# Which 128 rows of the input one load brings in: 16 images by 8 rows each, or 128 neighbouring rows of one stride

## The chip, the core and the metric

The kernel runs on one core of a Trainium2 chip. The metric is the device time of one execution, in microseconds (us); lower is better. The core has a matrix engine (PE), a vector engine (DVE), a scalar engine (ACT), GpSimd (POOL) and a queue engine (SP), which issues most of the transfers. Sixteen DMA engines move the data.

## The reference

The input is x, 128 images of 12 channels of 224 x 224 float32. What is computed, cut to what matters here:

```
pooled = x.reshape(B, 12, 14, 16, 14, 16).sum(axis=(3, 5))      # 16 x 16 patches
h = einsum('bcij,ce->bije', pooled, channel_weights)            # 196 tokens of 192 per image
h = h + attention(layernorm(h))       # 64 query tokens on the other 132
h = h + mixture_of_experts(layernorm(h))   # 8 experts, top 2, and a shared one
```

All of x (308 MB) is read once, and only its patch sums are used after that. The output is 128 x 196 x 192 float32.

## The kernel before, in words

**Groups and tiles.** The images go in 8 groups of 16 (`GB`). One group has 16 x 12 x 14 strips, a strip being 16 image rows of one channel, 3584 floats or 14,336 bytes that lie together in memory. A *unit* is (image, channel, half), where the half `s` says whether a strip is among the upper 7 or the lower 7 of its channel. Two neighbouring units, in the order (image, channel, half), lie 25,088 floats apart, over the border between channels and between images too. A *tile* is 128 units at one strip number `i` of 0 to 6: 128 partitions of 14,336 bytes, 1792 KB. A group has `TILES` = 21 tiles, numbered `t = 7k + i` with `k` of 0 to 2 (`CG`), 168 in all. Two buffers hold them (`xt`, `SLOTS` = 2).

**A tile's way.** `load` on SP issues tile t + 2 once DVE, ACT and POOL have all read tile t, which lies in the same buffer. Each of the three sums some of the tile's 14 patches: DVE in one reduction (`dve_tile`, L766), ACT patch by patch (`act_tile`, L626), POOL by a tree of additions (`pool_tile`, L556, L551, L562) that DVE finishes (`finish_rows`, L773). The sums go to `pooled[:, k, :]`.

**From sums to tokens.** Once all 21 tiles of a group are summed, PE transposes the three slices of `pooled` (item `tok`) and DVE copies them from PSUM to `Ptok`, laid out as unit (half, image) by channel. Item `V` multiplies the same slices by `blockG`, a block-diagonal matrix, built once before the groups from `bmask` (1 where a partition belongs to a unit column) and `repG` (`rep` says which channel a partition is). `rep` and `bmask` are made by POOL with memsets and affine selects. After this nothing depends on how a tile's rows were chosen.

**The order of the work.** First comes preparation of the weights (`PREP`), between which the tiles of group 0 are summed (`tiles_after`), one tile for each one or two steps. Then comes a pass for group 0's attention and gates, whose steps also take 19 tiles of group 1; `PLAN` lists the items of a step and `LATE0` its tile. Then each group's experts run in 63 steps on PE, DVE and ACT (`ffn_pe`, `ffn_dve`, `ffn_act`). In their gaps, by `PLAN`, stand the items of the next group, and by `EARLY` and `LATE` the tiles of that group and the one after. Each engine works its list strictly in order, so an engine that waits for a tile holds up the expert step behind it. SP's order is also fixed: it holds the loads, the stores of the output and, near the start, 8 + 9 small copies that spread the channel weights (`CWr_src`, `CWx`).

Of the kernel before, what the change touches and what calls it, by code (L numbers as in the profile page):

```python
# [31 lines left out]
NB, CH, IMG, PATCH = 128, 12, 224, 16  # L32
# [6 lines left out]
GB = 16  # L39
NG = NB // GB  # L40
CG = 3
HALF = NP // 2
HT = HALF * NP
UNITS = 2 * GB
# [179 lines left out]
def build(nc, x, cw, proj_w, proj_b, gate_w, gate_b, w1, w2, w3, sw1, sw2, sw3, out):  # L224
    ctx = ExitStack()
    with ctx:
# [28 lines left out]
        xt = sb("xt", [128, SLOTS, ROW])  # L255
# [16 lines left out]
        Ptok = sb("Ptok", [HT, UNITS, CH])  # L272
        V = sb("V", [HT, UNITS, CH + 1])
        val = sb("val", [HT, UNITS, CH + 1])
# [4 lines left out]
        PHT = sb("PHT", [128, 2, 4, HT])  # L279
# [11 lines left out]
        h = [ffn[:, i, :] for i in range(HR)]  # L291
# [21 lines left out]
        cres = h2q[0:UC, 4, :]  # L313
        CWcT = [rq[:, 0:3, :].rearrange("p a b -> p (a b)")[:, 0:CH], gs[:, 3, 0:CH]]
        G13 = sums[0:CH, :, :].rearrange("p a b -> p (a b)")[:, 0:CH + 1]
        rep = val[0:CH, :, :].rearrange("p a b -> p (a b)")[:, 0:CG * 128].rearrange("p (k n) -> p k n", k=CG)
        repG = gs[:, :, :].rearrange("p a b -> p (a b)")[:, 0:CG * (CH + 1)].rearrange("p (k c) -> p k c", k=CG)
        bmask = PHT[:, 0, 0, 0:UNITS]
        rmask = gt[0:8 * CH, 0, 0:8]
        wres = attw[0:CH, 2 * EX * INTER:2 * EX * INTER + 1024]  # L320

# [30 lines left out]
        pool_link = sem("pool_link")  # L352
        pe_passed, dve_passed = sem("pe_passed"), sem("dve_passed")

        xv = x.rearrange("(g b) (k c) (s i h) w -> g k i b (c s) (h w)", b=GB, k=CG, s=2, h=PATCH)


        PREP = [("CWcT", 0), ("CWcT", 1), ("G", 0), ("gate", 0), ("repG", 0), ("gate", 1)]
# [52 lines left out]
        @block.sync  # L411
        def _(sp):

            sp.dma_start(CWn, cw).then_inc(cw_in, 16)
            sp.wait_ge(const_done, 1)
            sp.dma_start(CW14[CH + 1:UC, :], proj_b.rearrange("(a d) -> a d", a=1)).then_inc(pb_in, 16)
            for k, (w, shared) in enumerate(((w1, sw1), (w3, sw3))):
                sp.dma_start(w13_nat[:, k * EX:k * EX + NE, :], w.rearrange("e i d -> i e d")).then_inc(w_in, 16)
                sp.dma_start(w13_nat[:, k * EX + NE, :], shared).then_inc(w_in, 16)
            for nat, a, b in ((w2_natA, 0, 128), (w2_natB, 128, D)):  # L420
                sp.dma_start(nat[:, 0:NE, :], w2[:, a:b, :].rearrange("e d i -> d e i")).then_inc(w_in, 16)
                sp.dma_start(nat[:, NE, :], sw2[a:b, :]).then_inc(w_in, 16)
            sp.dma_start(pw_natA, proj_w[0:128, :]).then_inc(w_in, 16)
            sp.dma_start(pw_natB, proj_w[128:D, :]).then_inc(w_in, 16)
            sp.dma_start(g_nat, gate_w).then_inc(w_in, 16)
            sp.dma_start(gbias[:, :], gate_b.partition_broadcast(128)).then_inc(gb_in, 16)
            for t in range(SLOTS):
                sp.dma_start(xt[:, t, :], xv[0, t // HALF, t % HALF]).then_inc(x_in[t], 16)
            sp.wait_ge(cwc_ready, 1)
            for b in range(8):  # L430
                sp.dma_start(CWr_src[b * CH:(b + 1) * CH, :], CW14[0:CH, :]).then_inc(cwr_in, 16)
            sp.wait_ge(cwx_split, 1)
            for s in range(SPL):
                for q in range(SPL):
                    a = (s * SPL + q) * UC
                    sp.dma_start(CWx[a:a + UC, :], CSP[:, s, :]).then_inc(cwx_in, 16)

            def load(g, t):

                for s in (dve_summed, act_summed, pool_read):  # L440
                    wait(sp, s, g.at(TILES, t - SLOTS + 1))
                slot = g.slot(t)
                sp.dma_start(xt[:, slot, :], xv[g.num(), t // HALF, t % HALF]).then_inc(x_in[slot], 16)

            def store(g, c):

                query, col, n = CHUNKS[c]
                st = stage[:, (g.par + c) % 2, :, :]
                done = out_stored[(g.par + c) % 2]
                if query:  # L450
                    sp.wait_ge(evac_dve, g.at(4, 2 * c + 2))
                else:
                    sp.wait_ge(evac_act, g.at(EVAC[-1], EVAC[c]))
                og = out.rearrange("(g b) t d -> g b t d", b=GB)[g.num()]
                for t in range((n + 127) // 128):
                    if query:
                        b0 = (col + 128 * t) // NQ
                        dst = og[b0:b0 + 2, 0:NQ, :]
                    elif n == 512:
                        dst = og[4 * t:4 * t + 4, NQ + col // GB:NQ + col // GB + 32, :]  # L460
                    else:
                        dst = og[:, TOK - 4:TOK, :]
                    sp.dma_start(dst, st[0:min(n, 128), t, :]).then_inc(done, 16)  # L463

            def load_after(g, t):

                if t + SLOTS < TILES:
                    load(g, t + SLOTS)
                elif g.k is not None or g.off < NG - 1:
                    load(g.plus(1), t + SLOTS - TILES)  # L470

            def ffn_dma(g, left):
                for step in range(STEPS):
                    c, e = divmod(step, EX)
                    for gt_, t in tiles_at(g, step, left):
                        load_after(gt_, t)
                    if e == 3 and c > 0:
                        store(g, c - 1)
                store(g, NCH - 1)

            for t in range(TILES):
                load_after(G(None, 0), t)
            for step in range(A_FIRST, STEPS):
                for gt_, t in tiles_at(G(None, -1), step):
                    load_after(gt_, t)
            ffn_dma(G(None, 0), 2)
            with sp.Fori(0, 2) as k:
                for off in (1, 2):
                    ffn_dma(G(k, off), 2)
            ffn_dma(G(None, 5), 2)  # L490
            ffn_dma(G(None, 6), 1)
            ffn_dma(G(None, 7), 0)
            for s in range(2):
                sp.wait_ge(out_stored[s], sum(TT) * 16 * NG // 2)
# [3 lines left out]
        def _(pool):  # L498
            links = [0]

            def link(ins):
                links[0] += 1
                ins.then_inc(pool_link, 1)
                pool.wait_ge(pool_link, links[0])
# [4 lines left out]
                                         base=0, pattern=[[-1, 128]], channel_multiplier=1))  # L509
            nc.gpsimd.tensor_copy(identb[:, :], ident[:, :]).then_inc(const_done, 1)  # L510
            nc.gpsimd.memset(mhalf[:, :], -0.5)
            for k in range(CG):
                link(nc.gpsimd.memset(rep[:, k, :], 0.0))

                link(nc.gpsimd.affine_select(out=rep[:, k, :].rearrange("p (b c s) -> p b c s", b=GB, c=4),
                                             in_=rep[:, k, :].rearrange("p (b c s) -> p b c s", b=GB, c=4),
                                             compare_op=ALU.not_equal, fill=1.0, base=-4 * k,
                                             pattern=[[0, GB], [-1, 4], [0, 2]], channel_multiplier=1))
            link(nc.gpsimd.memset(bmask, 0.0))
            for c in range(4):  # L520

                link(nc.gpsimd.affine_select(out=bmask.rearrange("p (s b) -> p s b", s=2),
                                             in_=bmask.rearrange("p (s b) -> p s b", s=2),
                                             compare_op=ALU.not_equal, fill=1.0, base=-2 * c,
                                             pattern=[[-1, 2], [-8, GB]], channel_multiplier=1))

            link(nc.gpsimd.memset(rmask, 1.0))
            link(nc.gpsimd.affine_select(out=rmask, in_=rmask, compare_op=ALU.is_ge, fill=0.0, base=0,
# [218 lines left out]
        def _(dve):  # L747
            links = [0]
            v = nc.vector
# [57 lines left out]
            def prep(r):  # L807
# [20 lines left out]
                if PREP[r][0] == "repG":  # L828
                    dve.wait_ge(prep_dve, P_DVE_N[r])
                    dve.wait_ge(const_done, 3)  # L830
                    for k in range(CG):
                        plink(v.tensor_tensor(
                            out=blockG[:, k, :].rearrange("p (u c) -> p u c", u=UNITS),
                            in0=bmask.unsqueeze(2).to_broadcast([128, UNITS, CH + 1]),
                            in1=repG[:, k, :].unsqueeze(1).to_broadcast([128, UNITS, CH + 1]), op=ALU.mult))

            def spread_cwc():
# [45 lines left out]
            def item(g, kind, i):  # L883
# [4 lines left out]
                if kind == "fin":  # L888
                    finish_rows(g, TILES - 1, *share(g, TILES - 1)["pool"])
                elif kind == "tok":  # L890
                    for k in range(CG):
                        ins = v.tensor_copy(
                            Ptok[:, :, 4 * k:4 * k + 4].rearrange("p (s b) c -> p s b c", s=2),
                            ps[0:HT, 128 * k:128 * k + 128].rearrange("p (b c s) -> p s b c", b=GB, c=4))
                    ins.then_inc(aux_dve, 1)
                elif kind == "stats":
                    links[0] = 0
                    dve.wait_ge(aux_dve, g.at(BYDVE[-1], BYDVE[R[("tok", 0)]]))
# [249 lines left out]
        def _(pe):  # L1148
# [3 lines left out]
            for r, (kind, i) in enumerate(PREP):  # L1152
# [14 lines left out]
                elif kind == "repG":  # L1167
                    pe.wait_ge(prep_dve, P_DVE_N[P_AT[("G", 0)]])
                    pe.wait_ge(const_done, 3)
                    for k in range(CG):  # L1170
                        last = mm(ps[:, k * (CH + 1):(k + 1) * (CH + 1)], rep[:, k, :], G13, start=True, stop=True)
                elif kind == "gate":
                    pe.wait_ge(w_in, 11 * 16)
                    n = 128 if i == 0 else 64
# [259 lines left out]
```

## Time and profile before

| | us |
|---|---|
| median of 3 runs | 2015.14 |
| lowest and highest run | 2013.2, 2017.29 |
| span of the profiled execution, first to last instruction | 2012.1 |

The profiled execution has its span as its only time; it is 3.0 us under the median of the runs. Over that span PE is busy for 1664.4 us (83%), DVE 1245.5, ACT 904.3 and POOL 653.7. A busy PE is not a PE at its peak: matmuls are pipelined and their ends are modelled. The DMA queue of SP moved 330.51 MB, and the mean over the span was 166 GB/s.

### The profile page before, as it was taken

What the parts mean: (1) busy time and instruction counts of PE and PEld (TensorE: products, weight loads), DVE (VectorE), ACT (ScalarE), POOL (GpSimd) and SP (SyncE); (2) the same over time, 40 slices, a digit from 0 to 9 for tenths busy, and PEclk for the clock granted to TensorE, in tenths of its full rate; (3) what the DMA queues carried; (4) which work ended last, traced back from release to release, by engine and by line L of the source; (5) the groups of instructions that cost most, each with busy time, mean ns of one, the idle gap of its engine ahead of it and who ended that gap; (6) DMA issues with size and microseconds to landing.
All of it is one profiled execution on the core that took longest, in us unless ns stands there. A gap on an engine that the chain in (4) does not pass through costs nothing.

```text
span 2012.1 us, 31811 instructions
## 1 busy us (share of the span) xinstructions
PE 1664.4 (83%) x9798; PEld 1269.1 (63%) x9798; DVE 1245.5 (62%) x2360; ACT 904.3 (45%) x2999; POOL 653.7 (32%) x735
## 2 busy tenths in 40 slices
PE   1430454699989998999889998999899989999998
PEld 1110342477667866786667766786677768877876
DVE  4453445576767667856757675856775675367355
ACT  1222333346644665365625664466546653533122
POOL 3222422353435343633344343524353432000000
PEclk9965565799999999999999999998999999999999
DMA  9999999888889788888978889878897980000000
GB/s 215 220 211 220 213 213 206 182 182 190 200 208 198 179 196 200 194 188 184 205 166 180 197 191 207 191 178 191 205 199 172 218 198 23 14 10 25 8 18 24
DMA packets 55455, 333.14 MB, mean 166 GB/s; under 512 B 4237, under 2 KB 33666, under 8 KB 33774
## 3 DMA queue, kind: packets, MB, share of 16 engines
q1 hardware_dynamic: 55062, 330.51, 73.2%
q8 instruction: 83, 1.36, 0.3%
q14 instruction: 94, 0.77, 0.1%
q10 hardware_dynamic: 216, 0.50, 0.1%
HBM read 311.10 MB, written 19.27 MB: 164 GB/s over the span
## 4 chain that ended last, share of the span: by engine, by line
PE 27%; issue 24%; DMA 21%; POOL 12%; DVE 7%; SPq 4%; ACT 3%; POOLq 0%; DVEq 0%; ACTq 0%
DMA xt<-in_x 21%; PE bank L1369 11%; PE bank L1217 7%; POOL kh_sum L556 6%; POOL kh_sum L551 4%; SPq L463 3%; PE bank L1391 3%; DVE pooled L766 3%; PE bank L1396 2%; ACT xt L626 1%; POOL row_sum L562 1%; PE bank L1312 1%; DVE ffn L1122 1%; POOL stat L568 1%; PE bank L1324 1%
## 5 line engine op out<-in xcount | busy, mean ns | idle before, releaser
L1369 PE MATMUL bank<-W2T,ffn 128*128 128x192 f32 (+1 forms) x3600 | 699.3, 333 | 15.7 <-DVE stage L1104 11.0
L1369 PEld LDWEIGHTS bank<-W2T,ffn 128*128 128x128 f32 (+1 forms) x3600 | 604.8, 191 | 72.8 <-DVE stage L1104 13.6
L556 POOL TENSOR_TENSOR kh_sum<-xt 128x768 f32<-128x768 f32 (+2 forms) x168 | 247.1, 1471 | 973.2 <-DMA xt<-in_x 966.8
L1122 DVE TENSOR_TENSOR ffn<-bank,ffn 128x512 f32<-128x512 f32 (+1 forms) x448 | 278.1, 621 | 386.2 <-PE bank L1217 166.5
L626 ACT ACTIVATE xt<-xt 128x256 f32<-128x256 f32 x776 | 313.1, 409 | 358.6 <-DMA xt<-in_x 358.4
L728 ACT ACTIVATE ffn<-bank 128x512 f32<-128x512 f32 (+1 forms) x504 | 273.3, 545 | 332.3 <-PE bank L1391 163.2
L766 DVE TENSOR_REDUCE pooled<-xt 128x1 f32<-128x256 f32 (+2 forms) x168 | 233.6, 1390 | 153.3 <-DMA xt<-in_x 152.3
L1132 DVE TENSOR_TENSOR ffn<-bank,ffn 128x512 f32<-128x512 f32 (+1 forms) x448 | 279.4, 624 | 40.4 <-DVE ffn L1122 33.3
L1391 PE MATMUL bank<-tokT,Wx 126*128 126x512 bf16 (+1 forms) x720 | 252.9, 355 | 20.6 <-ACT ffn L728 16.7
L551 POOL TENSOR_TENSOR kh_sum<-kh_sum 128x384 f32<-128x384 f32 (+2 forms) x336 | 231.1, 688 | 26.3
L1396 PE MATMUL bank<-cwT,sel 128*128 128x512 bf16 (+1 forms) x448 | 164.6, 367 | 25.8 <-DVE ffn L1132 24.9
L1217 PE MATMUL bank<-x0h,WT0h 128*128 128x512 f32 x288 | 156.4, 543 | 6.6 <-issue 5.9
L626 ACT ACTIVATION_READ_ACCUMULATOR xt<-xt 128x1 f32 x776 | 149.4, 193 | 0.0
L1391 PEld LDWEIGHTS bank<-tokT,Wx 126*128 126x128 bf16 x720 | 72.9, 102 | 79.3 <-ACT ffn L728 30.2
L1217 PE MATMUL bank<-x0h,WT0l 128*128 128x512 f32 x288 | 115.6, 402 | 0.0
L1217 PE MATMUL bank<-x1h,WT1s 128*128 128x512 f32 x288 | 115.4, 401 | 0.0
L1217 PE MATMUL bank<-x0l,WT0h 128*128 128x512 f32 x288 | 115.1, 400 | 0.0
L1217 PE MATMUL bank<-x1l,WT1s 128*128 128x512 f32 x288 | 114.9, 399 | 0.0
L1396 PEld LDWEIGHTS bank<-cwT,sel 128*128 128x128 bf16 x448 | 44.2, 99 | 104.9 <-DVE ffn L1132 54.7
L668 ACT ACT_TABLE_LOAD x28 | 35.9, 1283 | 106.6 <-PE bank L1273 53.8
L1312 PE MATMUL bank<-Msb,CWr 128*128 128x192 f32 x384 | 74.9, 336 | 0.0
L1119 DVE TENSOR_TENSOR ffn<-bank,ffn 128x512 f32<-128x512 f32 (+1 forms) x56 | 34.8, 621 | 54.0 <-ACT ffn L728 28.1
(253 smaller groups left out, 2164.6 us busy)
## 6 DMA issues: line engine op xcount, KB each, us to landing
xt<-in_x SPq DMA_DIRECT2D x168, 1792.0 KB, 13.9
out<-stage SPq DMA_DIRECT2D x192, 96.0 KB
ffn<-in_L_ffn_w SPq DMA_DIRECT2D x2, 768.0 KB
attw<-in_L_ffn_w SPq DMA_DIRECT2D x1, 512.0 KB
Wx<-tokT ACTq DMA_DIRECT2D x9, 54.2 KB
out<-stage SPq DMA_DIRECT2D x8, 48.0 KB
attw<-in_L_ffn_w SPq DMA_DIRECT2D x1, 256.0 KB
ffn<-in_L_ffn_sw SPq DMA_DIRECT2D x2, 96.0 KB
```

Of the source, the lines that this page charges most:

```text
L551: nc.gpsimd.tensor_tensor(out=out, in0=in0, in1=in1, op=ALU.add).then_inc(tree_step, 1)
L556: nc.gpsimd.tensor_tensor(out=kh, in0=src[:, 0:8, :], in1=src[:, 8:16, :], op=ALU.add).then_inc(pool_read, 1)
L626: last = nc.scalar.activation(src[:, :, j, :], src[:, :, j, :], ACT.Copy, accum_out=pooled[:, t // HALF, at:at + 1])
L728: nc.scalar.activation(silu[p][:, 0:n], h_ps(step, 0)[:, 0:n], ACT.Silu).then_inc(silu_done, 1)
L766: v.tensor_reduce(out=pooled[:, t // HALF, at + lo:at + hi], in_=src[:, lo:hi, :, :], axis=AX.XY, op=ALU.add).then_inc(dve_summed, 1)
L1122: v.tensor_tensor(out=gated[p][:, 0:n], in0=h_ps(step, 1)[:, 0:n], in1=silu[p][:, 0:n], op=ALU.mult).then_inc(gated_done, 1)
L1132: v.tensor_tensor(out=h[step % HR][:, 0:n], in0=cw_ps[:, 0:n], in1=gated[p][:, 0:n], op=ALU.mult).then_inc(h_done, 1)
L1217: ins = mm(o, left[q], right[q], start=(q == 0), stop=(q == len(left) - 1))
L1312: last = mm(ps[:, 0:D], CWr[:, q, i % 4, :], Msb[:, i // 4, D * q:D * q + D], start=False, stop=(q == 2))
L1369: last = mm(o, h[step % HR][:, 128 * t:128 * t + m], W2T[:, e, :], start=(e == 0 and query and t % 2 == 0), stop=(e == NE), skip_group_che ...
L1391: last = mm(o[:, 0:n], Wx[:, w:w + INTER], X2T[g.par][:, col:col + n], start=True, stop=True)
L1396: mm(cw_ps[:, 0:n], sel[:, e, :], cwT[:, at:at + n], start=True, stop=True).then_inc(cw_ready, 1)
```

## The change

A tile is now 128 neighbouring units of one stride, at one strip number. Tile `k` of a strip number holds units 128k to 128k + 127 in the order (image, channel, half), so 5 1/3 images with all their channels, where it held 16 images with 4 channels. The number of loads, their size, their order and the order in which tiles are summed stay.

```
-        xv = x.rearrange("(g b) (k c) (s i h) w -> g k i b (c s) (h w)", b=GB, k=CG, s=2, h=PATCH)
+        xv = x.rearrange("(g b) c (s i h) w -> g i (b c s) (h w)", b=GB, s=2, h=PATCH)
+
+        def x_rows(num, t):
+            k, i = t // HALF, t % HALF
+            return xv[num, i, 128 * k:128 * k + 128, :]
...
-                sp.dma_start(xt[:, slot, :], xv[g.num(), t // HALF, t % HALF]).then_inc(x_in[slot], 16)
+                sp.dma_start(xt[:, slot, :], x_rows(g.num(), t)).then_inc(x_in[slot], 16)
```

The masks follow. `rep` is filled by one memset and one select over 384 columns instead of three of each over 128. `bmask` gets three slices of 32 columns, since a partition's unit column now depends on `k`, and 12 selects instead of 4:

```
+            link(nc.gpsimd.memset(rep, 0.0))
+            link(nc.gpsimd.affine_select(out=rep.rearrange("p (b c s) -> p b c s", b=GB, c=CH),
...
-            for c in range(4):
+            for c in range(CH):
...
-                                             pattern=[[-1, 2], [-8, GB]], channel_multiplier=1))
+                                             pattern=[[128, CG], [-1, 2], [-2 * CH, GB]], channel_multiplier=1))
```

And the copy of the tokens is one copy instead of three:

```
-                    for k in range(CG):
-                        ins = v.tensor_copy(
-                            Ptok[:, :, 4 * k:4 * k + 4].rearrange("p (s b) c -> p s b c", s=2),
-                            ps[0:HT, 128 * k:128 * k + 128].rearrange("p (b c s) -> p s b c", b=GB, c=4))
-                    ins.then_inc(aux_dve, 1)
+                    v.tensor_copy(Ptok[:, :, :].rearrange("p (s b) c -> p s b c", s=2),
+                                  ps[0:HT, 0:CG * 128].rearrange("p (b c s) -> p s b c", b=GB, c=CH)).then_inc(aux_dve, 1)
```

In the order of SP's instructions the change shows in the form of the loads. These are SP's first rows in the program before, from the loads of the expert weights to the first stores; sizes are those of the destination, `in_x` is x, `ffn`, `attw` and `h2q` are places of the weights.

```order
L418 DMA ffn<-in_L_ffn_w 128x8x192
L421 DMA attw<-in_L_ffn_w 128x8x128
L423 DMA h2q<-in_L_attn_proj_w 128x192
L428 DMA xt<-in_x 128x1x3584 x2
L431 DMA Msb<-CW 12x192 x8
L436 DMA CWx<-SPT 14x192 x9
L443 DMA xt<-in_x 128x1x3584 x47
```

And these are the same places of SP in the changed program.

```order
L423 DMA ffn<-in_L_ffn_w 128x8x192
L426 DMA attw<-in_L_ffn_w 128x8x128
L428 DMA h2q<-in_L_attn_proj_w 128x192
L433 DMA xt<-in_x 128x3584 x2
L436 DMA Msb<-CW 12x192 x8
L441 DMA CWx<-SPT 14x192 x9
L448 DMA xt<-in_x 128x3584 x47
```

Nothing moved. The destination of an x load was cut as 128 x 1 x 3584 to go with a source of three sizes, 16 x 8 x 3584; now source and destination both have the two sizes 128 x 3584. The weight loads above them have 128 as the first size of source and of destination in both programs.

POOL's rows from the first mask to the memset of `sel`, before; `val` holds `rep`, `PHT` holds `bmask`, `gt` holds another mask.

```order
L513 MEMSET val 12x128
L515 AFFINE_SELECT val<-val 12x128
L513 MEMSET val 12x128
L515 AFFINE_SELECT val<-val 12x128
L513 MEMSET val 12x128
L515 AFFINE_SELECT val<-val 12x128
L519 MEMSET PHT 128x32
L522 AFFINE_SELECT PHT<-PHT 128x32 x4
L527 MEMSET gt 96x8
```

The same stretch of POOL in the changed program.

```order
L517 MEMSET val 12x384
L519 AFFINE_SELECT val<-val 12x384
L523 MEMSET PHT 128x3x32
L526 AFFINE_SELECT PHT<-PHT 128x3x32 x12
L531 MEMSET gt 96x8
```

Four instructions fewer for `rep`, eight selects more for `bmask`, each on three times the columns; all that POOL does later, the wait of PE for `const_done` among it, stands behind them.

## Rows read from the trace of the kernel before

**Rows 1.** The page: busy time of each engine.
```profile
PE 1664.4 (83%) x9798; PEld 1269.1 (63%) x9798; DVE 1245.5 (62%) x2360; ACT 904.3 (45%) x2999; POOL 653.7 (32%) x735
```

**Rows 2.** The page: tenths of the span in 40 slices of 50.3 us.
```profile
PE   1430454699989998999889998999899989999998
PEclk9965565799999999999999999998999999999999
DMA  9999999888889788888978889878897980000000
GB/s 215 220 211 220 213 213 206 182 182 190 200 208 198 179 196 200 194 188 184 205 166 180 197 191 207 191 178 191 205 199 172 218 198 23 14 10 25 8 18 24
```

**Rows 3.** Stretches: length, busy PE, PEld, DVE, ACT, POOL; PEclk, DMA share, GB/s.
```profile
23.00:200.00 177.00, 48.66 (x132) 18.07 (x132) 82.77 (x104) 37.98 (x174) 37.01 (x84) 0.77 1.00 216
203.00:374.00 171.00, 71.74 (x413) 52.36 (x412) 84.91 (x157) 58.57 (x251) 49.62 (x83) 0.56 0.98 211
369.00:1646.00 1277.00, 1190.54 (x7178) 917.44 (x7179) 871.48 (x1699) 685.49 (x2291) 533.58 (x518) 0.97 0.85 192
1646.00:1842.00 196.00, 194.13 (x1214) 152.98 (x1213) 116.38 (x253) 80.75 (x204) 23.18 (x15) 0.99 0.12 31
```

**Rows 4.** The chain that ended last, 25 to 62 us: start us, us, what.
```profile
25.70 16.46 DMA xt<-in_x
42.18 2.30 DVE pooled L766
44.49 14.64 DMA xt<-in_x
59.15 2.30 DVE pooled L766
61.47 14.33 DMA xt<-in_x
```

**Rows 5.** Loads of x: the issuing line, and their time to landing.
```profile
L443 SPq DMA_DIRECT2D xt<-in_x x166: 536/544/3814, 25.7 to 1650.7; - x166
...
DMA to landing us min/median/max: 10.7/13.9/20.0
```

**Rows 6.** The DMA view of 4 to 10 us, 40 slices, weight loads alone.
```profile
GB/s 369 374 369 374 379 369 374 369 384 343 328 333 328 323 338 328 328 328 328 328 323 328 328 328 328 328 328 328 307 336 311 316 319 321 300 290 294 294 283 297
DMA packets 2922, 1.99 MB, mean 332 GB/s; under 512 B 64, under 2 KB 2922, under 8 KB 2922
```

**Rows 7.** Waits of DVE, then of ACT, 23 to 200 us: us, times, longest.
```profile
DVE pooled L766 <- DMA xt<-in_x: 93.7, 20, 7.8
...
ACT xt L626 <- DMA xt<-in_x: 147.1, 21, 15.6
```

**Rows 8.** The same waits, 203 to 374 us.
```profile
DVE pooled L766 <- DMA xt<-in_x: 38.8, 12, 6.9
...
ACT xt L626 <- DMA xt<-in_x: 71.5, 17, 8.9
```

**Rows 9.** The last gate instruction, one for each group: the first, seventh and eighth.
```profile
L1083 DVE TENSOR_TENSOR CS<-gt,CS x1: 366/366/366, 368.5 to 368.5; 128x200 bf16<-128x200 f32 x1
...
L1083 DVE TENSOR_TENSOR CS<-gt,CS x1: 1751/1751/1751, 1646.4 to 1646.4; 128x200 bf16<-128x200 f32 x1
...
L1083 DVE TENSOR_TENSOR CS<-gt,CS x1: 355/355/355, 1841.7 to 1841.7; 128x200 bf16<-128x200 f32 x1
```

**Rows 10.** Waits for x loads, 369 to 1646 us.
```profile
ACT xt L626 <- DMA xt<-in_x: 136.2, 63, 5.5
DVE pooled L766 <- DMA xt<-in_x: 19.7, 16, 2.9
```

**Rows 11.** The masks on POOL, by line; PE and DVE behind them, in order of time.
```profile
L515 POOL TENSOR_SCALAR_AFFINE_SELECT val<-val x3: 778/779/781, 2.4 to 4.8; 12x128 f32<-12x128 f32 x3
L522 POOL TENSOR_SCALAR_AFFINE_SELECT PHT<-PHT x4: 213/224/326, 5.9 to 7.1; 128x32 f32<-128x32 f32 x4
16.64 1.42 PE L1171 MATMUL bank<-sums,val 12*128 12x13 f32 x6 [1.26 <-POOL PH L541]
23.13 2.29 DVE L766 TENSOR_REDUCE pooled<-xt 128x8 f32<-128x2048 f32 x1 [7.34 <-DMA xt<-in_x]
```

**Rows 12.** The token copy, and a DVE instruction of 98 x 384 from SBUF.
```profile
L892 DVE COPY Ptok<-bank x24: 278/279/293, 203.7 to 1674.5; 98x128 f32<-98x128 f32 x24
L900 DVE TENSOR_TENSOR val<-Ptok,V x8: 546/554/848, 207.6 to 1680.4; 98x384 f32<-98x384 f32 x8
```

More of the change, by code:

```diff
@@ L315, in build @@
         G13 = sums[0:CH, :, :].rearrange("p a b -> p (a b)")[:, 0:CH + 1]
-        rep = val[0:CH, :, :].rearrange("p a b -> p (a b)")[:, 0:CG * 128].rearrange("p (k n) -> p k n", k=CG)
+        rep = val[0:CH, :, :].rearrange("p a b -> p (a b)")[:, 0:CG * 128]
         repG = gs[:, :, :].rearrange("p a b -> p (a b)")[:, 0:CG * (CH + 1)].rearrange("p (k c) -> p k c", k=CG)
-        bmask = PHT[:, 0, 0, 0:UNITS]
+        bmask = PHT[:, 0, 0:CG, 0:UNITS]
         rmask = gt[0:8 * CH, 0, 0:8]
@@ L427, in _ @@
             for t in range(SLOTS):
-                sp.dma_start(xt[:, t, :], xv[0, t // HALF, t % HALF]).then_inc(x_in[t], 16)
+                sp.dma_start(xt[:, t, :], x_rows(0, t)).then_inc(x_in[t], 16)
             sp.wait_ge(cwc_ready, 1)
@@ L511, in _ @@
             nc.gpsimd.memset(mhalf[:, :], -0.5)
-            for k in range(CG):
[L513 to L518, printed above, removed]
+            link(nc.gpsimd.memset(rep, 0.0))
+            link(nc.gpsimd.affine_select(out=rep.rearrange("p (b c s) -> p b c s", b=GB, c=CH),
+                                         in_=rep.rearrange("p (b c s) -> p b c s", b=GB, c=CH),
+                                         compare_op=ALU.not_equal, fill=1.0, base=0,
+                                         pattern=[[0, GB], [-1, CH], [0, 2]], channel_multiplier=1))
             link(nc.gpsimd.memset(bmask, 0.0))
-            for c in range(4):
-                link(nc.gpsimd.affine_select(out=bmask.rearrange("p (s b) -> p s b", s=2),
-                                             in_=bmask.rearrange("p (s b) -> p s b", s=2),
+            for c in range(CH):
+                link(nc.gpsimd.affine_select(out=bmask.rearrange("p k (s b) -> p k s b", s=2),
+                                             in_=bmask.rearrange("p k (s b) -> p k s b", s=2),
                                              compare_op=ALU.not_equal, fill=1.0, base=-2 * c,
-                                             pattern=[[-1, 2], [-8, GB]], channel_multiplier=1))
+                                             pattern=[[128, CG], [-1, 2], [-2 * CH, GB]], channel_multiplier=1))
             link(nc.gpsimd.memset(rmask, 1.0))
@@ L833, in prep @@
                             out=blockG[:, k, :].rearrange("p (u c) -> p u c", u=UNITS),
-                            in0=bmask.unsqueeze(2).to_broadcast([128, UNITS, CH + 1]),
+                            in0=bmask[:, k, :].unsqueeze(2).to_broadcast([128, UNITS, CH + 1]),
                             in1=repG[:, k, :].unsqueeze(1).to_broadcast([128, UNITS, CH + 1]), op=ALU.mult))
@@ L890, in item @@
                 elif kind == "tok":
-                    for k in range(CG):
-                        ins = v.tensor_copy(
-                            Ptok[:, :, 4 * k:4 * k + 4].rearrange("p (s b) c -> p s b c", s=2),
-                            ps[0:HT, 128 * k:128 * k + 128].rearrange("p (b c s) -> p s b c", b=GB, c=4))
-                    ins.then_inc(aux_dve, 1)
+                    v.tensor_copy(Ptok[:, :, :].rearrange("p (s b) c -> p s b c", s=2),
+                                  ps[0:HT, 0:CG * 128].rearrange("p (b c s) -> p s b c", b=GB, c=CH)).then_inc(aux_dve, 1)
                 elif kind == "stats":
@@ L1170, in _ @@
                     for k in range(CG):
-                        last = mm(ps[:, k * (CH + 1):(k + 1) * (CH + 1)], rep[:, k, :], G13, start=True, stop=True)
+                        last = mm(ps[:, k * (CH + 1):(k + 1) * (CH + 1)], rep[:, 128 * k:128 * k + 128], G13, start=True, stop=True)
                 elif kind == "gate":
```

## The prediction

> **What bounds the kernel now.** I read the page's slices first. In the first seven (352 us) the DMA engines are nine tenths busy or more while PE is at six tenths or less; from the ninth on PE stands at eight or nine tenths and the DMA digit is mostly 8 [rows 2]. So there are two regimes: before the first experts start (about 374 us) the loads of x set the time, after it the expert steps do. PE's 1664.4 busy us of 2012.1 [rows 1] hide that split.
>
> The stretches say the same. From 23 to 200 us (group 0's tiles beside the preparation) DMA share is 1.00 at 216 GB/s and DVE is busy for 82.8 of 177 us. [...]
>
> The chain of waits shows the cycle: a load of 14 to 16 us, then DVE's reduction of 2.3 us, which frees the buffer for the next load [rows 4]. From 42.18 to 59.15 us is 16.97 us for two tiles (two buffers take turns), 8.49 us each. A tile is 1.835 MB, and 1.835 MB / 8.49 us = 216 GB/s. So the DMA engines never pause; the loads queue behind each other, and the latency does not set the rate. The shortest landing is 10.7 us [rows 5]; less the 8.5 us of moving, 2.2 us is fixed.
>
> **What the change does to a load.** Size, count and the 14,336-byte run of a row stay. What changes is how source and destination are cut: 16 x 8 rows against 128 x 1 before, 128 against 128 now. The trace before has loads of the second kind: the expert weights, 128 as first size on both sides, on the same queue and engines. While they moved, in packets all under 2 KB (768-byte rows for the first), the rate was 369 to 384 GB/s in the first nine slices and mostly 328 in the next [rows 6], against 211 to 220 for x in its undisturbed slices [rows 2], though x has runs 19 times as long. Something other than the engines holds x at 0.58 of that rate (216/374). Two things differ between the kinds: the shape that spreads rows over engines and partitions, and where in memory the rows lie. The change alters the first, and the second only in part (rows still 100,352 bytes apart).
>
> I take it to be the shape. [...] So the new rate is at best that of rows 6: 1.835 MB / 0.375 MB per us = 4.9 us for a tile. The bound below is 8.5 us, no change. I take 4.9 (by the slices at 328 it would be 5.6), since rows 6 are the nearest of the new form and longer packets should not lose to short ones.
>
> [...]
>
> **What a faster tile is worth, stage by stage.**
>
> *Stage A, tiles 2 to 20 of group 0.* SP reaches tile 2's load at 25.7 us, behind 17 small copies; this stays, since the chain of waits starts there [rows 4]. Tiles 0 and 1 land earlier, for nothing. Now 19 tiles take until about 197 us, 9.0 us each with start-up. Then: a buffer's own cycle is 2.2 + 4.9 + 2.3 (DVE) + 0.5 (issue, [rows 5]) = 9.9 us for two tiles, 4.95 each, so latency and moving bind together at about 4.9. Above it lies what DVE does between tiles: 82.8 us of work for 21 tiles, 3.9 each, in strict order with PE's preparation. DVE now waits for loads 93.7 us and ACT 147.1 [rows 7]; without all of DVE's the stretch would be 83 us, too few for the loads. When preparation stands between a landing and its reduction, the buffer is freed 1 or 2 us late; every 0.5 us of that for each tile is 9.5 us. Between 5.1 and 6.6 us a tile I take 5.8: 25.7 + 2.2 + 19 x 5.8 = 138 against 197: **59 us saved** (44 to 72).
>
> *Stage B, 203 to 374 us.* Here items of a long dependent chain alternate with tiles. DVE waits 38.8 us for loads, ACT 71.5 [rows 8]. The floor is 19 tiles x 4.95 = 94 us, the stretch without DVE's load waits 171 - 39 = 132, and without ACT's, if each held up the rest, 100. ACT's waits hide partly behind DVE's. I take 121: **50 us saved** (25 to 70).
>
> *Stage C, 369 to 1646 us, six groups of experts.* The last gate instructions [rows 9] give 1277.9 us for six groups, 213.0 each; the seventh, which has almost no tiles, takes 195.3. So all that tiles cost here, work and waits, is 17.7 us a group, 106 us in six: the bound above. Its parts, by group: DVE 871.5/6 - 116.4 = 28.9 busy us, ACT 685.5/6 - 80.8 = 33.5 [rows 3], and waits for loads (136.2 + 19.7)/6 = 26.0 [rows 10]. Only the last goes away, and with in-order engines I share by size: 26.0/88.4 = 0.29 of 106 = **31 us saved** (0 to 80). POOL's far longer waits cost nothing, since nobody waits for it but the loads.
>
> *Masks.* `rep`: three memset-select pairs become one on 384 columns, 0.78 to 2.34 us against 3 x 0.78. `bmask`: 12 selects on 96 columns instead of 4 on 32; 0.22 us each as now to 0.67 [rows 11]. POOL is 0 to 6 us later, about 2.5. PE waits for POOL here before its matmuls at 16.6 us, but their user on DVE stands behind tile 0's reduction at 23.1 us [rows 11], so 4 us or more lie free. Tile 0 may now land at 19.7 us; then up to 2 us shows, before 25.7, when SP is still busy with copies. Cost 0; without that cover 2 us.
>
> *Token copy.* Three copies of 0.279 us become one of 98 x 384, near 0.55 [rows 12]: 0.3 us a group, 2 us in all at most, mostly beside PE work. I count 0 to 1.
>
> *Issue.* The load's issue at 0.54 us may shorten with the simpler shape; it lies in the cycle of stage A, where the engines bind as well. Counted at 0.
>
> Sum: 59 + 50 + 31 + 1 = 141 us. 2012.1 - 141 = 1871, and with the 3.0 us from span to median, **1874 us**.
>
> **The rivals.**
>
> *1. Something else in line binds stages A and B* (chance 0.13). The loads do come at 4.9 us, but the chains of PE, DVE and ACT that the waits now hide take over: PE at its lower clock in both. Then A saves 40, B 25 and C nothing or little: 2015 - 70 = 1945. For it: DVE's 85 busy us in 171 of stage B mean a chain with few idle hands. Against it: DVE's 20 waits in A are 4.7 us each on average and no other work of its own fills them [rows 7].
>
> *2. The rate does not change* (0.09). If reading rows 100,352 bytes apart is what holds x to 216 GB/s, both forms have it, and only masks and copies change: 2015, within 0.2%. For it: the weights lie packed, x does not. Against it: the rate stands so flat at 211 to 220 over seven slices that differ in images and channels.
>
> [...]
>
> *3. The loads get slower* (0.05). Sixteen images spread over 38 MB become 5 1/3 images in 13 MB; if engines then meet more often in the same part of memory, a tile takes longer. It decides at once: 40 tiles before the experts make 0.1 us a tile 4 us, 0.2%. At a rate a tenth lower, 9.4 us a tile, it is 40 x 0.9 = 36 us: 2051. Stage C would still cover it, 21 x 9.4 = 197 of 213 us.
>
> *4. The experts gain more* (0.04): waits for late tiles drive most of the 106 us of stage C, and 80 or more come back: 2015 - 200 = 1815.
>
> **How the numbers follow.** My forecast has 0.69, the rivals 0.13, 0.09, 0.05, 0.04. Without a change of rate nothing here is worth 0.2% (4 us), which is about what a measurement can tell. Faster: 0.69 + 0.13 + 0.04 = 0.86; same 0.09; slower 0.05. The range leaves out rivals 2 and 3 and half of 4 (0.16) and a tail of the forecast: from A 72, B 70, C 60 together, 1813, rounded to 1815, to rival 1's 1945 with a little over, 1950.
>
> **What would show it.** In the new profile: GB/s of 300 or more in the first slices; shortest landing near 7 us and median 8 to 9; the last gate instruction of the first group at about 260 us instead of 368.5, and six groups in about 1247 us instead of 1277.9; DVE's waits for loads before 374 us down from 132 to under 40 us. Wrong would be: landings still at 13.9 (rival 2), or landings at 8 with the first gates later than 300 us (rival 1). If the groups of experts speed up by over 60 us together, the share that I gave the waits is wrong.

## The result

The changed kernel takes 1879.03 us (median of 4 runs, 1868.31 to 1881.75) against 2014.17 us before (4 runs, 2011.46 to 2017.29): a ratio of 0.932, 95% interval 0.9292 to 0.9349. The profiled execution took 1880.6 us, its span 1878.9. The forecast was 1874.

### The profile page after: what moved, and what is told of

Same layout as the page of the kernel before. It is cut to its first block, busy times and chain, and to the rows that moved or that the text cites. A ratio compares the mean times of both kernels' runs of the same rounds, so it can differ in the third digit from the quotient of the medians.

```text
span 1878.9 us, 31672 instructions
## 1 busy us (share of the span) xinstructions
PE 1634.6 (87%) x9665; PEld 1260.1 (67%) x9798; DVE 1239.9 (66%) x2344; ACT 905.8 (48%) x2999; POOL 657.5 (35%) x739
## 3 DMA queue, kind: packets, MB, share of 16 engines
q1 hardware_dynamic: 55062, 330.51, 47.6%
## 4 chain that ended last, share of the span: by engine, by line
PE 69%; DVE 14%; issue 7%; DMA 6%; ACT 2%; POOL 1%; SPq 1%; DVEq 0%; ACTq 0%; another core or an unknown queue 0%; POOLq 0%
PE bank L1370 25%; PE bank L1218 19%; DMA xt<-in_x 6%; PE bank L1392 6%; PE bank L1397 3%; DVE pooled L770 2%; PE bank L1285 2%; DVE ffn L1123 2%; PE bank L1313 2%; DVE ffn L1133 2%; PE bank L1325 2%; PE bank L1274 1%; PE bank L1280 1%; PE bank L1297 1%; PE bank L1290 1%
## 5 line engine op out<-in xcount | busy, mean ns | idle before, releaser
L1397 PE MATMUL bank<-cwT,sel 128*128 128x512 bf16 (+1 forms) x315 | 110.0, 349 | 27.4 <-DVE ffn L1133 27.0
L1397 PEld LDWEIGHTS bank<-cwT,sel 128*128 128x128 bf16 x448 | 43.8, 98 | 115.8 <-DVE ffn L1133 66.8
```

What stands on the lines that cost most here:

```text
L1397: mm(cw_ps[:, 0:n], sel[:, e, :], cwT[:, at:at + n], start=True, stop=True).then_inc(cw_ready, 1)
```

## The profile after

The page of the changed kernel, its slices (now 47.0 us each) and its load of x:

```profile
span 1878.9 us, 31672 instructions
PE   1714639999999989998999989998999999999998
DMA  8896755546554465555455455556554530000000
GB/s 304 315 352 239 289 219 196 205 165 222 205 204 182 172 222 216 180 200 207 175 205 204 168 215 204 182 198 223 195 205 174 210 131 10 10 18 18 9 19 26
xt<-in_x SPq DMA_DIRECT2D x168, 1792.0 KB, 7.3
```

PE comes to nine tenths in the seventh slice, where it took until the ninth (longer) one before [rows 2]. The first three slices move 304 to 352 GB/s where it was 211 to 220. Beside the experts the DMA digit fell from about 8 to about 5: the same 330.51 MB of SP's queue take 47.6% of the 16 engines' span, where they took 73.2% of a longer one.

By line, the load and its time to landing:

```profile
L448 SPq DMA_DIRECT2D xt<-in_x x166: 327/333/1939, 25.3 to 1517.4; - x166
DMA to landing us min/median/max: 6.5/7.3/11.9
```

Against 10.7/13.9/20.0 before [rows 5], the shortest landing lost 4.2 us. Less the 2.2 us that the prediction took as fixed, 4.3 us of moving are left for 1.835 MB, an estimate of 427 GB/s. The median lost 6.6 us, 2.4 more than the shortest; that a load now queues less behind the other would explain it, but was not measured by itself.

The chain that ended last, at the place of [rows 4]:

```profile
25.27 6.85 DMA xt<-in_x
...
32.15 2.30 DVE pooled L770
...
34.46 7.90 DMA xt<-in_x
...
42.38 2.30 DVE pooled L770
```

The cycle of a buffer is 10.2 us from 32.15 to 42.38, where it was 16.97.

The milestones: the reduction of group 0's last tile, in order of time, first before and then after; and by line the last gate instruction of the first, seventh and eighth group after, to set beside [rows 9].

```profile
196.81 2.29 DVE L766 TENSOR_REDUCE pooled<-xt 128x8 f32<-128x2048 f32 x1 [5.94 <-DMA xt<-in_x]
```

```profile
132.04 2.29 DVE L770 TENSOR_REDUCE pooled<-xt 128x8 f32<-128x2048 f32 x1 [2.50 <-DMA xt<-in_x]
L1084 DVE TENSOR_TENSOR CS<-gt,CS x1: 510/510/510, 271.9 to 271.9; 128x200 bf16<-128x200 f32 x1
L1084 DVE TENSOR_TENSOR CS<-gt,CS x1: 354/354/354, 1516.0 to 1516.0; 128x200 bf16<-128x200 f32 x1
L1084 DVE TENSOR_TENSOR CS<-gt,CS x1: 356/356/356, 1708.3 to 1708.3; 128x200 bf16<-128x200 f32 x1
```

| stage | before | after | saved | forecast |
|---|---|---|---|---|
| A, start to group 0's last tile | 196.8 | 132.0 | 64.8 | 59 |
| B, to the first group's last gate | 171.7 | 139.9 | 31.8 | 50 |
| C, six groups | 1277.9 | 1244.1 | 33.8 | 31 |
| the rest | 365.7 | 362.9 | 2.8 | 1 (copy) |
| span | 2012.1 | 1878.9 | 133.2 | 141 |

These are stages of one execution each, and the 2.8 us of the rest are within what two executions of one kernel differ by. Four of the experiments below have fast loads in A and B too (far rows, halves by columns, 64 x 2, and the fast load before the experts only): their last tile comes at 135.2 to 136.9 us and their first gate at 275.0 to 276.2. So A is worth 60 to 65 us, and B takes 139 to 140 us in all five.

## The experiments

Each is the changed kernel with one edit. "Before" is the kernel before on the same chip; the experiments ran on three chips, where its medians were 2008.7, 2010.1 and 2011.4 us. Two theories of the rate are open at first: the **shape** of the transfer (how source and destination are cut), or the **place** of the rows in memory. A third, that it is SP's issue path, came up when the load's issue was seen to fall from 0.54 to 0.33 us.

**The old cut on rows at the new place.**

```
-            return xv[num, i, 128 * k:128 * k + 128, :]
+            return xv[num, i, 72 * k:72 * k + 144, :].rearrange("(a b) w -> a b w", b=9)[:, 0:8, :]
```

> The changed kernel, but with its load cut as before: source 16 x 8 x 3584, destination 128 x 1 x 3584. So that the two sizes of rows cannot be merged, each run of 8 neighbouring units is followed by one that is left out; the tile spans 144 units (14.5 MB), nearly where the changed kernel's lie. It sums other rows than the reference does. If the shape sets the rate: landings near 13.9 us, about 215 GB/s in the first slices, 2010 to 2020 us. If where the rows lie in memory sets it: landings near 7.3 us and 1870 to 1885 us.

2012.52 us (10 runs), ratio 1.0031 (1.0011 to 1.005). Its slices and its landing:

```profile
GB/s 218 220 207 219 213 217 206 186 184 198 196 204 191 177 206 199 192 192 183 207 164 191 196 188 206 192 181 198 204 197 174 213 200 21 13 10 25 9 17 24
DMA to landing us min/median/max: 10.8/14.1/19.8
```

The whole gain is gone, with rows of the same stride as in the changed kernel but for one in nine that is left out. The tiles begin 72 units apart here and not 128, so they overlap, and the last quarter of a group's units is not read.

**The new cut on rows far apart.**

```
+        xfar = x.rearrange("b c (s i h) w -> i (c s) b (h w)", s=2, h=PATCH)
-            return xv[num, i, 128 * k:128 * k + 128, :]
+            return xfar[i, 3 * num + k]
```

> The changed kernel, load 128 x 3584 on both sides, but the 128 rows are one strip of each of the 128 images, 2,408,448 bytes apart, so a tile is spread over all of x. It sums other rows than the reference does. If the shape sets the rate: landings near 7.3 us, 1870 to 1885 us. If the spread in memory sets it: slower loads, 9 to 14 us to landing, 1900 to 2020 us.

1875.65 us (4 runs), ratio 0.9348 (0.9314 to 0.9382); by its view of the tile:

```profile
DMA to landing us min/median/max: 6.4/7.3/12.3
```

Rows 24 times as far apart cost nothing that these runs resolve: the median landing is 7.3 us in both, and the ratio's interval overlaps that of the changed kernel. The two runs together rule the place out, over the distances tried.

**Masks and copy without the loads.**

```
+        xold = x.rearrange("(g b) (k c) (s i h) w -> g k i b (c s) (h w)", b=GB, k=CG, s=2, h=PATCH)
-            return xv[num, i, 128 * k:128 * k + 128, :]
+            return xold[num, k, i]
```

> Loads of before (16 images by 8 rows, 16 x 8 on 128 x 1), with the masks and the token copy of the changed kernel, so the tokens are mixed up. If the loads are the whole effect: within 0.2% of before, 2010 to 2018 us, token copy 0.56 us instead of 3 x 0.279. If masks or copy were worth something: 2 us or more off on either side, the masks up to 3 us slower.

2010.6 us (10 runs), ratio 1.0016 (0.9999 to 1.0033). The rest is worth nothing or a loss of up to 0.3%. In order of time, PE's wait for the masks:

```profile
19.53 1.42 PE L1174 MATMUL bank<-sums,val 12*128 12x13 f32 x6 [4.31 <-POOL PH L547]
```

It starts 2.9 us later than before [rows 11], as costed. In the changed kernel, where tile 0's reduction is over at 20.7 us, DVE waits 0.28 us for these matmuls, and tile 2's load starts at 25.3 us all the same. The copy takes 0.548 us instead of 3 x 0.279.

**A longer issue by a build switch.** Rows and sizes are those of the changed kernel.

```
     nc = bacc.Bacc("TRN2", target_bir_lowering=False, num_devices=1)
+    nc.dge_precook = False
```

> [...] If sizes of rows and partitions set the rate: landings 7.3 to 7.6 us, and the end at most 5 us later, 1877 to 1886 us. If it is the issue path that deals the rows out better: landings near 13.9 and about 2014 us.

1883.4 us (4 runs), ratio 0.9395 (0.936 to 0.9431). Its issue of a load and its landing:

```profile
L448 SPq DMA_DIRECT2D xt<-in_x x166: 471/478/2174, 28.5 to 1515.5; - x166
DMA to landing us min/median/max: 6.8/7.6/12.8
```

Landings stay short (7.6 us at the median) with an issue of 0.478 us instead of 0.333, so the issue is not the cause (64 x 2, below, has 0.542 and lands at 7.7). The time is 7.8 us over that of the far rows on the same chip, though the two intervals just overlap. Tile 2's load starts at 28.5 us instead of 25.3, because transfers ahead of it have longer issues too: those of the expert weights in `ffn` take 0.668 us at the median instead of 0.423, those of tiles 0 and 1 0.602 instead of 0.432, and tile 0's starts at 13.8 us instead of 10.9. The small copies keep theirs (0.714 us to `Msb`, 0.746 to `CWx`, in both runs). The first group's last gate comes at 278.8 us, where it is at 271.9 in the changed kernel and at 275.0 to 276.2 in the four other runs with fast loads. That cost lies in SP's list as a whole, not in the form of the x loads.

**Halves of a tile by rows, and by columns.** Two transfers for a tile in both; the semaphore's targets are doubled.

```
+                for a in (0, 64):
+                    sp.dma_start(xt[a:a + 64, slot, :], x_rows(g.num(), t)[a:a + 64, :]).then_inc(x_in[slot], 16)
```

> The changed kernel with each tile loaded by two transfers, partitions 0 to 63 and then 64 to 127, both with 64 x 3584 on either side. [...] If engines slow one another where neighbouring partitions are written, so that half of the partitions offer half of the write ways: about 215 GB/s and landings of 11 us or more, 1990 to 2030 us, although source and destination are cut alike. If only unequal cuts of source and destination are slow: 1880 to 1890 us.

```
+                for a in (0, ROW // 2):
+                    sp.dma_start(xt[:, slot, a:a + ROW // 2], x_rows(g.num(), t)[:, a:a + ROW // 2]).then_inc(x_in[slot], 16)
```

> The changed kernel with each tile loaded by two transfers of all 128 rows, the first and the second half of each row's columns (7,168-byte runs). It is the control for the halves by rows: as many transfers and the same bytes. By every theory at full rate, 1875 to 1890 us; if two transfers for a tile cost by themselves: 1900 us or more.

By rows: 2044.18 us (2 runs), ratio 1.0171 (1.0146 to 1.0196), which is over the 1990 to 2030 that I expected: the halves by rows are slower than the kernel before, and why by so much stays open. By columns: 1874.51 us (2 runs), ratio 0.9327 (0.9308 to 0.9345). The slices of the two, rows first:

```profile
GB/s 212 215 206 212 209 215 204 183 180 189 182 196 194 172 197 193 199 183 174 203 164 187 189 184 200 197 171 194 195 192 186 182 201 54 16 11 21 12 18 24
```

```profile
GB/s 297 315 324 238 296 252 162 201 175 236 191 209 195 173 228 206 192 207 209 175 206 205 173 251 179 199 170 230 187 205 175 216 126 10 12 17 18 9 19 26
```

Source and destination are cut alike in both. So an unequal cut is not needed for a slow load: 64 partitions from 0 or from 64 are slow too, 204 to 215 GB/s in the first seven slices where the halves by columns have up to 324.

**Another 64 partitions: 32 to 95.**

```
-                sp.dma_start(xt[:, slot, :], x_rows(g.num(), t)).then_inc(x_in[slot], 16)
+                sp.dma_start(xt[32:96, slot, :], x_rows(g.num(), t)[32:96, :]).then_inc(x_in[slot], 16)
```

> The changed kernel, but every load from tile 2 on brings only the 64 rows of partitions 32 to 95, cut as 64 x 3584 on both sides; the other 64 partitions keep the rows of tiles 0 and 1, so half of the input is never read. As many rows and engines as one of the halves by rows, whose shortest landing was 6.7 us (2.2 fixed and 4.5 of moving, 0.92 MB at about 205 GB/s). If what halves the rate is that partitions 0 to 63, or 64 to 127, offer only half of the write ways, then 32 to 95, half from each side, go at full rate: shortest landing 4.4 to 5.0 us. If 64-row transfers are slow by themselves: 6.5 us or more.

The landing times are the verdict here (the total, 1847.62 us, has half the bytes), first for the halves by rows, then for the halves by columns, which are as many transfers of as many bytes, then for partitions 32 to 95:

```profile
DMA to landing us min/median/max: 6.7/11.5/19.4
```

```profile
DMA to landing us min/median/max: 4.4/6.3/12.3
```

```profile
DMA to landing us min/median/max: 4.7/5.0/12.0
```

The medians can't be compared, since two halves of a tile queue behind each other; the shortest landings can. The same number of rows, cut alike, is 2.0 us quicker to land when its partitions come half from each side. Less 2.2 us, 0.92 MB moves in 2.5 us against 4.5: an estimate of 367 against 204 GB/s. So for loads of 64 rows it is the partitions written that set the rate, by two shortest landings, 6.7 and 4.7 us; why they do, no run shows.

**A finer unequal cut.**

```
+            return xv[num, i, 48 * k:48 * k + 192, :].rearrange("(a b) w -> a b w", b=3)[:, 0:2, :]
```

> The changed kernel with the source cut as 64 x 2 x 3584 (every third unit left out, so that the sizes cannot be merged; it sums other rows than the reference does) and the destination as 128 x 1 x 3584. If any unequal cut gives each of the 16 engines 8 neighbouring partitions: slow as 16 x 8, 2000 to 2020 us. If 16 as the first size was special: something between, or 1875 to 1890 us.

1879.61 us (2 runs), ratio 0.9352 (0.9333 to 0.9371), where I had expected 2000 to 2020 if any unequal cut is slow:

```profile
L448 SPq DMA_DIRECT2D xt<-in_x x166: 534/542/2207, 25.7 to 1516.5; - x166
DMA to landing us min/median/max: 6.8/7.7/11.6
```

So of the two unequal cuts tried, 64 x 2 on 128 x 1 is nearly as fast as equal sizes and only the coarse 16 x 8 is slow. It also bounds the issue time: here the x loads alone have the long issue of 0.54 us, and the ratio is 0.003 (some 6 us) over that of the changed kernel, with intervals that overlap. So the shorter issue may be worth a few us; no run shows that it is.

**The fast load before the experts only.**

```
+            if isinstance(num, int) and num < 2:
+                return xv[num, i, 128 * k:128 * k + 128, :]
+            return xv[num, i, 72 * k:72 * k + 144, :].rearrange("(a b) w -> a b w", b=9)[:, 0:8, :]
```

> The changed kernel, but groups 2 to 7 load by the slow cut, source 16 x 8 x 3584 with every ninth unit left out (these groups sum other rows than the reference does). It keeps the gain before the first experts and gives up the one beside them. By the traces (97 us sooner at the first group's last gate, 34 us over the six groups after it): 1879 + 34 = about 1913 us, 1903 to 1923. If the experts' own gain came from something else than their loads: 1880 to 1890 us.

1912.68 us (4 runs), ratio 0.952 (0.9503 to 0.9536): about seven tenths of the gain (4.8% of 6.8%) comes from two groups of loads out of eight. In its trace the first group's last gate comes at 275.0 us and the seventh's at 1547.1, so the six groups take 1272.1 us, against 1277.9 before and 1244.1 after, and ACT's and DVE's waits for tiles in that stage are back (156.7 and 26.0 us).

**Two ways to gain more.** Other shares of a tile in the first 40 tiles, and nine small copies issued by ACT instead of SP:

```
-SHARE0 = {"dve": (0, 8), "act": (8, 12), "pool": (12, NP)}
+SHARE0 = {"dve": (0, 6), "act": (6, 10), "pool": (10, NP)}
```

> The changed kernel with other shares of a tile in the first 40 tiles: DVE sums 6 patches instead of 8, ACT 4 as before, POOL 4 instead of 2. DVE's reduction falls from 2.29 to about 1.73 us. If the buffer's own cycle (landing, DVE, issue) binds group 0's tiles and DVE's order binds the pass after them: 19 x 0.28 = 5 us and up to 19 x 0.56 = 11 us less, 1863 to 1875 us. If POOL's longer reading (1.0 us instead of 0.73) and tree, or the dependent chain of the items, bind: within 3 us of the changed kernel.

```
+                if r == P_AT[("CWcT", 1)]:
+                    act.wait_ge(cwx_split, 1)
...
+                            act.dma_start(CWx[a:a + UC, :], CSP[:, s, :]).then_inc(cwx_in, 16)
```

> The changed kernel with the nine small copies to CWx issued by ACT, which waits then for tile 0, instead of SP. SP reaches tile 2's load at about 18.5 us, and the buffer is free at 20.7 instead of 25.3 when it is issued now. If the first wait of the loads is on the path: 4 to 5 us less, 1872 to 1876 us. If preparation on DVE, which takes from 25.7 to 31.7 us, sets the time there: 0 to 2 us less.

> The changed kernel with both: shares of 6, 4 and 4 patches, and the nine copies on ACT. If the two save time at different places, their gains add: 1860 to 1871 us; if one hides the other, it is no faster than the better of them.

The shares: 1870.83 us (6 runs), ratio 0.9297 (0.9269 to 0.9324). The copies: 1872.93 us (5 runs), 0.9314 (0.929 to 0.9338). Both: 1872.83 us (6 runs), 0.9307 (0.9287 to 0.9328). All three intervals overlap that of the changed kernel, 0.9292 to 0.9349, so none is shown to beat it, though all beat the kernel before. In the trace of the shares the first group's last gate comes at 265.5 us, 6.4 us sooner than in the changed kernel and some 10 us sooner than in the four other runs with fast loads there; the totals don't resolve it. With the copies moved, the load of tile 2 starts at 21.5 us, but DVE reads the tile no earlier, in order of time:

```profile
31.89 0.17 DVE L829 TENSOR_TENSOR gT1s<-bank,gT1s 64x8 fp32r<-64x8 f32 x1
32.09 2.29 DVE L771 TENSOR_REDUCE pooled<-xt 128x8 f32<-128x2048 f32 x1
```

It used to wait 0.40 us for the tile at 32.15; now preparation on DVE ends just then.

## Why the prediction was right, and where it was not

**The rate of a load: right, and a little low.** It rested on weight loads of the new form at 369 to 384 GB/s [rows 6], 4.9 us a tile. The shortest landing implies 4.3 us, an estimate of 427 GB/s for rows of 14,336 bytes, so the rate of the weight loads, in packets under 2 KB, was a lower bound and not the value.

**That the shape, not the place, sets it: right.** The old cut at the new place gives the old time, the new cut at a far place the new time. Before the runs it was an estimate: rows 6 show a faster load of the new form, not what makes it faster. What slows a load cut 16 x 8 is still not shown. Loads of 64 rows are fast or slow by which partitions they write (landings from 4.7 and from 6.7 us), but no run moves the partitions of the old load, and the profile has no record of which engine wrote which partition. One of my expectations had 64 x 2 as slow as 16 x 8, and it is fast (shortest landings 6.8 and 10.8 us); 32 x 4, which lies between them, was not run.

**Stage A, 59 forecast, 64.8 measured.** The term of 5.8 us a tile was a little high: (132.0 - 27.9) / 19 = 5.5, and 5.7 in the four other runs.

**Stage B, 50 forecast, 31.8 measured: the term that was mis-sized.** I stood between 39, what DVE waited for loads, and 71, what ACT waited, and took 50. The waits for loads that are left, first from 18 to 150 us, then from 150 to 272 us (stage A's last tile is read at 132 us; the next, at 145 us, was waited for by neither engine):

```profile
ACT xt L630 <- DMA xt<-in_x: 82.4, 20, 10.8
DVE pooled L770 <- DMA xt<-in_x: 30.3, 15, 4.7
```

```profile
ACT xt L630 <- DMA xt<-in_x: 27.7, 9, 7.8
DVE pooled L770 <- DMA xt<-in_x: 7.8, 3, 4.0
```

In stage A DVE's waits fell from 93.7 us [rows 7] to 30.3, by 63.4, ACT's from 147.1 to 82.4, by 64.7, and the stage by 64.8: either engine would have priced it. In stage B DVE's fell from 38.8 us [rows 8] to 7.8, by 31.0, ACT's from 71.5 to 27.7, by 43.8, and the stage by 31.8. So the step that failed is the allowance of 11 us beyond DVE's waits: ACT's longer waits brought nothing on top, and even DVE's 39 did not all go. Loads make up 23.6% of the chain that ended last there, where they were 56.6%; the rest of it is the items of the dependent chain on PE, DVE and ACT. That ACT's waits lay beside that chain is argued from this; no run moved work between ACT and DVE to test it. With two patches of a tile moved from DVE to POOL the stage took 134.9 us (130.6 to 265.5), 5 less in that one execution, so DVE's own work is part of what sets it.

**Stage C, 31 forecast, 33.8 measured.** After 272 us no wait of ACT or DVE for a tile is left of the 155.9 us before [rows 10]. So 22% of their waiting was worth time; DVE's waits alone, 19.7 us, would have priced this stage too low. The run with slow loads from group 2 on confirms the order of size: its median is 1912.7 - 1879.0 = 34 us longer (on another chip), its ratio 0.020 higher, which is 40 us, and its six groups take 1272.1 - 1244.1 = 28 us longer. The share by which I split the 106 us was a guess at a proportion, and its closeness is no proof of the rule.

**Masks, copy and issue: right.** Masks and copy alone are within 0.3%. For the issue time, counted at nothing, the run of 64 x 2 leaves room for a few us and shows none. The masks' range was too narrow by its own terms (12 x 0.67 - 4 x 0.22 = 7.2 us later at most, not 6); the 2.9 us measured are near its middle value.

**The rivals.** Rival 1, that another chain takes over, gave 25 us for stage B, nearer to the 31.8 measured than my 50, and 40 for stage A, where 64.8 came back and loads are still 59.5% of the chain that ended last. So it holds in good part for B and not for A. That the rate stays (rival 2), or falls (rival 3), is refuted. Rival 4's 1815 counts 90 us for stage C; with the 80 it names it would be 1825.

**The total.** 1879.0 lies close to the forecast of 1874 in part by luck: stage B came 18 us short, A some 6 over, and C and the rest nearly 5 over.

## What to carry to other kernels

Compare the rate of a kernel's large loads with its best other load before believing that the memory is the bound: here weight loads with rows a nineteenth as long went at 369 to 384 GB/s at best, about 1.7 times the 211 to 220 of x, and the DMA engines looked fully busy in both. Where a load fills 128 partitions, give source and destination the same first size of 128, or at least compare a source cut into 16 pieces with it (median landings here: 7.3 us with equal sizes, 13.9 with 16 pieces, 7.7 with 64), and don't load partitions 0 to 63 and 64 to 127 as separate transfers (2044 us here, 1875 as halves by columns). The longest wait is a poor price for a stage: in stage B the time that came back was what DVE's waits lost, not ACT's. That is one stage; in A both fit, and in C neither.

## What the runs showed of the hardware that was not expected

A stretch of the changed kernel, with the columns of [rows 3]:

```profile
25.00:132.00 107.00, 43.69 (x128) 16.94 (x128) 75.39 (x96) 32.77 (x151) 33.16 (x74) 0.80 0.90 334
```

The busy share of the DMA engines does not tell their rate: it is 0.90 at 334 GB/s here, and was 1.00 at 216 GB/s before [rows 3]. Loads cut 16 x 8 on 128 x 1 ran at about half the rate of 64 x 2 on 128 x 1: the shortest landings are 10.8 and 6.8 us, less 2.2 us an estimate of 213 and 399 GB/s. Halving a tile by partitions cost 170 us over halving it by columns (2044 against 1875). The issue on SP takes 0.33 us for 128 x 3584 on both sides instead of 0.54 for the unequal cuts. Equal sizes alone don't give that: 64 x 3584 on both sides took 0.47 us in the halves by rows and 0.52 for partitions 32 to 95.
